# Moving the query normalisation from VectorE to ScalarE, a maximum to GpSimd, and re-timing a software-pipelined attention step

## The reference, cut to what matters

```python
def _layernorm(x, axis=-1, eps=1e-05):
    m = mean(x); v = var(x)
    return (x - m) / sqrt(v + eps)
...
scores = einsum('bhqd,bhkd->bhqk', q, k) * (1 / sqrt(16))   # q = layernorm(x), k = v = context
attn = softmax(scores, axis=-1)
out = einsum('bhqk,bhkd->bhqd', attn, v)
...
x = x + xattn(layernorm(x), ctx, ctx)
x = x + ffn(layernorm(x), w_gate, w_up, w_down)   # fp4_linear: w and x quantised by blocks of 16
```

## Time and profile before

| | |
|---|---|
| median of three timed runs | 544.02 us |
| profiled execution | 541.95 us, its span 540.2 us |
| TensorE clock granted, mean | 0.987 of full speed |
| busy: PE, weight loads | 494.7 us (92%), 396.8 us (73%) |
| busy: DVE, ACT, POOL | 453.2 (84%), 361.0 (67%), 269.9 us (50%) |
| chain that ended last | PE 57%, DVE 21%, issue 11%, SP queue 3% |

### The profile page before, as it was taken

How to read it: one execution, slowest core, us unless ns; L and a number is a source line. 1 busy time by engine, 2 the same in 40 slices (tenths; PEclk the granted TensorE clock), 3 DMA queues, 4 the chain that set the end, 5 groups by cost and what they waited for, 6 DMA issues and landing times.

```text
span 540.2 us, 13895 instructions
## 1 busy us (share of the span) xinstructions
PE 494.7 (92%) x4105; PEld 396.8 (73%) x4132; DVE 453.2 (84%) x1175; ACT 361.0 (67%) x707; POOL 269.9 (50%) x391
## 2 busy tenths in 40 slices
PE   3759999999999999999886799999999999999996
PEld 2326666666666666665454699999999999999996
DVE  3668999999999999989655788888998888898764
ACT  3227888888888888887683356666556666656653
POOL 5203444554444544433415466676666666666543
PEclk9999999999999999999995999999999999999999
DMA  6795545454455544440000000000000000000000
GB/s 197 195 222 146 143 137 148 121 156 131 134 149 156 142 131 138 118 118 2 4 1 0 2 12 21 21 19 16 13 19 19 19 19 19 10 19 20 21 21 30
DMA packets 43799, 40.63 MB, mean 75 GB/s; under 512 B 4728, under 2 KB 43512, under 8 KB 43768
## 3 DMA queue, kind: packets, MB, share of 16 engines
q1 hardware_dynamic: 43768, 40.26, 26.6%
HBM read 10.55 MB, written 4.19 MB: 27 GB/s over the span
## 4 chain that ended last, share of the span: by engine, by line
PE 57%; DVE 21%; issue 11%; SPq 3%; POOL 2%; DMA 2%; ACT 2%; DVEq 1%; POOLq 0%; ACTq 0%
PE SC L1086 21%; PE PV L1086 12%; DVE MF L678 12%; PE PV L1037 4%; PE SC L1005 4%; PE T L1111 4%; PE MX L1019 4%; PE T L1116 2%; DVE stats L686 2%; DVE QN L699 2%; PE T L988 1%; PE SC L1111 1%; DMA QS<-QP 1%; SPq L291 1%; DVE MP L708 1%
## 5 line engine op out<-in xcount | busy, mean ns | idle before, releaser
L678 DVE TENSOR_REDUCE MF<-MX 128x2 f32<-128x512 f32 x256 | 167.4, 684 | 18.3 <-PE MX L1019 17.7
L531 ACT ACTIVATE P<-SC 128x512 f32<-128x512 f32 x256 | 142.6, 605 | 25.3 <-PE SC L1005 24.4
L1019 PE MATMUL MX<-KS,QS 96*128 96x256 bf16 x512 | 103.8, 287 | 10.2 <-DMA QS<-QP 5.4
L1005 PE MATMUL SC<-QS,KS 98*128 98x256 bf16 x512 | 99.6, 277 | 0.2 <-DMA QS<-MT 0.2
L480 POOL TENSOR_TENSOR HQ<-HN,hscale 128x704 f32<-128x704 f32 x31 | 43.1, 1391 | 60.7 <-DVE HN L835 60.7
L1037 PE MATMUL PV<-P,VA 128*32 128x256 f32 x1024 | 69.4, 389 | 2.7 <-ACT OT L540 0.8
L1019 PEld LDWEIGHTS MX<-KS,QS 96*128 96x128 bf16 x512 | 47.0, 100 | 32.5 <-DVE MF L678 18.6
L610 ACT ACTIVATE HH<-T 128x768 fp32r<-128x768 f32 x31 | 25.2, 813 | 67.0 <-PE T L1111 67.0
L1005 PEld LDWEIGHTS SC<-QS,KS 98*128 98x128 bf16 x512 | 43.7, 98 | 33.7 <-ACT P L531 13.6
L1086 PE MATMUL SC<-WH,XH 128*128 128x352 f32 x256 | 68.1, 348 | 0.0
L1086 PE MATMUL SC<-WH,XL 128*128 128x352 f32 x256 | 62.5, 326 | 0.0
(11 more groups left out here) (134 smaller groups left out, 1018.8 us busy)
## 6 DMA issues: line engine op xcount, KB each, us to landing
KS<-KP SPq DMA_DIRECT2D x96, 128.0 KB, 2.4
QS<-QP SPq DMA_DIRECT2D x96, 128.0 KB, 2.4
X<-in_x SPq DMA_DIRECT2D x16, 256.0 KB, 2.8
C<-in_ctx SPq DMA_DIRECT2D x16, 256.0 KB, 3.1
out<-OB SPq DMA_DIRECT2D x32, 128.0 KB, 1.7
W<-in_L_ffn_w_down SPq DMA_DIRECT2D x1, 704.0 KB, 6.2
W<-in_L_ffn_w_gate SPq DMA_DIRECT2D x1, 640.0 KB, 4.5
W<-in_L_ffn_w_up SPq DMA_DIRECT2D x1, 640.0 KB, 4.9
```

Source lines behind the costliest of these rows:

```text
L531: nc.scalar.activation(P[g % 2][:, j, :, :], SC[h % 3][:, :, :], ACT.Exp, scale=0.25).then_inc(exp_done, 1)
L678: nc.vector.tensor_reduce(MF[st.slot(off, 2)][:, :, h:h + 1], MX[h % 2][:, :, :], AX.X, ALU.max, negate=True).then_inc(mx_done, 1)
L1005: last = nc.tensor.matmul(SC[h % 3][:, k, :], KS[r][0:ROWS, h, k * 128:(k + 1) * 128], QS[r][0:ROWS, h, :], start=True, stop=True)
L1019: last = nc.tensor.matmul(MX[h % 2][:, q, :], QS[r][0:PROD, h, q * 128:(q + 1) * 128], KS[r][0:PROD, h, :], start=True, stop=True)
```

## The change

ACT normalises x as scale * x + bias with scale `rstd` and bias `qbias` = -mean * rstd; POOL makes `nmean` and `qbias`. POOL takes the maximum of `WC` with the constant. Statistics move from head (0,1) to (0,3) on DVE, the split of the maxima from (2,2) to (2,1), the weights' scales from (2,3) to (2,0), the second output half from (3,2) to (3,3). ACT makes the keys' second part at (0,3), the queries' parts at (1,3), (2,2) and (3,3), and the two `OT` copies at (0,3) and (2,1). PE's transposes and two of its `PV` groups move with them.

```diff
@@ -150,6 +150,7 @@
         rstd = [sb(f"rstd{r}", [128, QT]) for r in range(2)]
+        nmean, qbias = sb("nmean", [128, QT]), [sb(f"qbias{r}", [128, QT]) for r in range(2)]
         MF = [sb(f"MF{r}", [128, QT, H]) for r in range(2)]
@@ -196,7 +197,7 @@
         consts = sem("consts")
-        ve_ready, rstd_ready, qn_ready = sem("ve_ready"), sem("rstd_ready"), sem("qn_ready")
+        ve_ready, rstd_ready, qbias_ready, qn_ready = (sem(n) for n in ("ve_ready", "rstd_ready", "qbias_ready", "qn_ready"))
         stats_seq, var_ready, kn_ready, neg_ready = (sem(n) for n in ("stats_seq", "var_ready", "kn_ready", "neg_ready"))
@@ -414,8 +415,11 @@
                     nc.gpsimd.tensor_scalar(ve[r][:, :], mv[:, :, 1], EPS, None, ALU.add).then_inc(ve_ready, 1)
-                    pool.wait_ge(ve_ready, st.times(LEAD, 1, 1))
+                    nc.gpsimd.tensor_scalar(nmean[:, :], mv[:, :, 0], -1.0, None, ALU.mult).then_inc(ve_ready, 1)
+                    pool.wait_ge(ve_ready, st.times(LEAD, 2, 2))
                     nc.gpsimd.tensor_tensor(rstd[r][:, :], ve[r][:, :], mhalf[:, :], ALU.pow).then_inc(rstd_ready, 1)
+                    pool.wait_ge(rstd_ready, st.times(LEAD, 1, 1))
+                    nc.gpsimd.tensor_tensor(qbias[r][:, :], nmean[:, :], rstd[r][:, :], ALU.mult).then_inc(qbias_ready, 1)
                 if st.has(1):
@@ -427,6 +431,9 @@
                     ws = wslice(st, GRID)
+                    pool.wait_ge(w_abs, st.times(GRID, 1, 1))
+                    gate(pool)
+                    nc.gpsimd.tensor_scalar(WC[:, :], WC[:, :], MAGIC * ONE, None, ALU.max).then_inc(w_c, 1)
                     pool.wait_ge(w_c, st.times(GRID, 1, 1))
@@ -521,6 +528,15 @@
+            def normalise(st, q):
+
+                r, b = st.slot(LEAD, 2), st.item(LEAD)
+                act.wait_ge(qbias_ready, st.times(LEAD, 1, 1))
+                act.wait_ge(q_tr, st.times(LEAD, 3))
+                gate(act)
+                nc.scalar.activation(QN[:, q, :, :, :], by_parity(X1[:, bass.ds(b * (QT * D) + q * D, D)]), ACT.Identity,
+                                     bias=qbias[r][:, q:q + 1], scale=rstd[r][:, q:q + 1]).then_inc(qn_ready, 1)
+
             def exp(st, g, j):
@@ -540,8 +556,11 @@
             def first_step(st):
-                for parts, bank, n, tr, out in ((KP, TA, 0, k_tr, k_out), (KP, TA, 1, k_tr, k_out), (QP, TB, 0, q_tr, q_out),
-                                                (KP, TA, 2, k_tr, k_out), (QP, TB, 1, q_tr, q_out), (QP, TB, 2, q_tr, q_out)):
+                part_out(KP[0], TA, 0, k_tr, k_out, st)
+                for q in range(QT):
+                    normalise(st, q)
+                for parts, bank, n, tr, out in ((KP, TA, 1, k_tr, k_out), (QP, TB, 0, q_tr, q_out), (KP, TA, 2, k_tr, k_out),
+                                                (QP, TB, 1, q_tr, q_out), (QP, TB, 2, q_tr, q_out)):
                     part_out(parts[0], bank, n, tr, out, st)
@@ -551,20 +570,26 @@
                         exp(st, g, j)
-                        for n, at in enumerate(((0, 3), (1, 1), (1, 2))):
-                            if (g, j) == at and st.has(LEAD):
-                                part_out(KP[st.slot(LEAD, 2)], TA, n, k_tr, k_out, st)
+                        if (g, j) == (0, 3) and st.has(LEAD):
+                            part_out(KP[st.slot(LEAD, 2)], TA, 0, k_tr, k_out, st)
+                        if (g, j) == (0, 3) and st.has(-1):
+                            evacuate(st, -1, 1)
                         if (g, j) == (0, 3) and st.has(GRID):
...
                             nc.scalar.activation(WC[:, :], wslice(st, GRID), ACT.Abs, scale=MAGIC).then_inc(w_abs, 1)
-                        if (g, j) == (0, 2) and st.has(-1):
-                            evacuate(st, -1, 1)
-                        for n, at in enumerate(((2, 1), (2, 3), (3, 3))):
+                        if (g, j) == (0, 3) and st.has(LEAD):
+                            part_out(KP[st.slot(LEAD, 2)], TA, 1, k_tr, k_out, st)
+                        if (g, j) == (1, 1) and st.has(LEAD):
+                            for q in range(QT):
+                                normalise(st, q)
+                        if (g, j) == (1, 2) and st.has(LEAD):
+                            part_out(KP[st.slot(LEAD, 2)], TA, 2, k_tr, k_out, st)
+                        if (g, j) == (2, 1) and st.has(0):
+                            evacuate(st, 0, 0)
+                        for n, at in enumerate(((1, 3), (2, 2), (3, 3))):
                             if (g, j) == at and st.has(LEAD):
                                 part_out(QP[st.slot(LEAD, 2)], TB, n, q_tr, q_out, st)
-                        if (g, j) == (3, 1) and st.has(0):
-                            evacuate(st, 0, 0)
                         if st.first == B - 1 and HG * g + j < LOTS:
@@ -682,6 +707,8 @@
                 dve.wait_ge(loaded[rc], st.turn(LEAD, RING, 32))
+                dve.wait_ge(ve_ready, st.times(LEAD, 2))
+                gate(dve)
                 for q in range(QT):
@@ -690,16 +717,6 @@
                     nc.vector.bn_aggr(mv[:, q, :], stats[:, q, :]).then_inc(stats_seq, 1)
-
-            def normalise(st, q):
-
-                r, b = st.slot(LEAD, 2), st.item(LEAD)
-                dve.wait_ge(rstd_ready, st.times(LEAD, 1, 1))
-                dve.wait_ge(q_tr, st.times(LEAD, 3))
-                nc.vector.tensor_scalar(QN[:, q, :, :, :],
-                                        by_parity(X1[:, bass.ds(b * (QT * D) + q * D, D)]),
-                                        mv[:, q, 0:1], rstd[r][:, q:q + 1],
-                                        ALU.subtract, ALU.mult).then_inc(qn_ready, 1)
@@ -762,10 +779,6 @@
-            def round_weights(st):
-                dve.wait_ge(w_abs, st.times(GRID, 1, 1))
-                nc.vector.tensor_scalar(WC[:, :], WC[:, :], MAGIC * ONE, None, ALU.max).then_inc(w_c, 1)
-
             def weights_out(n):
@@ -776,33 +789,26 @@
                         maximum(st, g, j)
-                        if (g, j) == (0, 1) and st.has(LEAD):
+                        if (g, j) == (0, 3) and st.has(LEAD):
                             statistics(st)
-                        if (g, j) == (0, 1) and st.has(LEAD):
                             aggregate(st)
...
                             weight_maxima(st)
-                        if (g, j) == (2, 3) and st.has(SCALE):
-                            weight_limits(st)
-                        if (g, j) == (3, 1) and st.has(SCALE):
-                            weight_inverses(st)
-                        if (g, j) == (1, 0) and st.has(LEAD):
-                            normalise(st, 0)
-                        if (g, j) == (1, 0) and st.has(LEAD):
-                            normalise(st, 1)
-                        if (g, j) == (2, 2) and st.has(1):
+                        if (g, j) == (2, 1) and st.has(-1):
+                            denominators(st, 0)
+                            output(st, 0)
+                        if (g, j) == (2, 1) and st.has(1):
                             maxima_high(st)
...
                             maxima_out(st)
-                        if (g, j) == (2, 1) and st.has(-1):
-                            denominators(st, 0)
-                            output(st, 0)
-                        if (g, j) == (3, 2) and st.has(-1):
+                        if (g, j) == (2, 0) and st.has(SCALE):
+                            weight_limits(st)
+                        if (g, j) == (3, 3) and st.has(-1):
                             denominators(st, 1)
                             output(st, 1)
-                        if (g, j) == (1, 3) and st.has(GRID):
-                            round_weights(st)
+                        if (g, j) == (3, 1) and st.has(SCALE):
+                            weight_inverses(st)
                         if st.first == B - 1 and HG * g + j < LOTS:
@@ -1063,10 +1069,10 @@
                         max_scores(st, g, j)
-                        for n, at in enumerate(((0, 3), (1, 1), (1, 3))):
+                        for n, at in enumerate(((0, 1), (1, 0), (1, 3))):
                             if (g, j) == at and st.has(LEAD):
                                 keys(st, n)
-                        for n, at in enumerate(((1, 3), (2, 3), (3, 2))):
+                        for n, at in enumerate(((2, 0), (2, 3), (3, 1))):
                             if (g, j) == at and st.has(LEAD):
@@ -1077,7 +1083,7 @@
                             transpose_weights(HG * g + j)
-                        if (g, j) == ((0, 2), (1, 1), (2, 2), (3, 3))[g]:
+                        if (g, j) == ((0, 3), (1, 1), (2, 1), (3, 3))[g]:
                             values(st, g)
```

## The result

The changed kernel takes 553.1 us (median of four runs, 551.53 to 558.46) against 544.12: a ratio of 1.0171, 95% interval 1.0131 to 1.0212. It is 9 us slower, where 540.6 was forecast and 536.0 to 546.0 given as the range. Its profiled execution took 552.0 us, 10.05 more than that of before.

The account below looks back on a forecast made before the run. DVE and PE were both nearly full, with the bound passing to PE: 14.33 + 0.39 + 0.04 = 14.76 us a step against 15.02, 0.26 x 13 = 3.4 us off, forecast 540.6 us, range 536.0 to 546.0.

Parts of the forecast that it names:

- What bounds the kernel: Attention step: DVE and PE nearly full, PE's own work 14.33 us, its two waits for DVE 0.69 us a step.
- ACT, what comes: Two QN activations on ACT between the exponentials of heads 5 and 6, taken at 0.49 us each, 0.98 a step.
- rival 2: ACT reads x's strided columns slowly, about 0.2 us more a pass: 15.15 us a step, 545.7 us; chance 0.1.
- The step laid out: Attention step timed from head 0's score pair: QN at 6.23, PV at 8.88 behind exponential 7, end at 14.76 us.
- POOL: nmean, qbias (0.22 us each) and the WC maximum (0.64 us) on POOL are covered, with 7.07 busy of 15.02 us.
- SP: Nothing added to SP's queue; the DMA of MT behind the keys' six lands at 14.4 to 14.6, before 14.76 us.
- rival 3: The DMA of MT behind the keys' stack becomes the bound: 0.51 us more a step, 550.6 us; chance 0.1.
- the ends: First items and last steps of the attention part: change taken as zero, 1 us either way.
- The chances: Outcomes for the whole kernel: faster (below 538.6 us) 0.3, slower (above 549.5) 0.1, within 1% 0.6.

Follow-up runs that it names:

- e12: Kernel before with the WC maximum still on DVE but two heads earlier, at (1,1) instead of (1,3): 541.3 us, ratio 0.9950.
- e4: Kernel before with only the WC maximum moved from DVE to POOL: 541.0 us, ratio 0.9943.
- e2: Changed kernel with ACT reading x and writing QN in x's own column order (query columns come out misordered): 549.2 us, ratio 1.0111.
- e8: Changed kernel with the queries' three parts later on PE and ACT: 557.3 us, ratio 1.0261.
- e1: Changed kernel with statistics and mv on DVE back at head (0,1): 546.0 us, ratio 1.0025.
- e7: e4 with the split of the maxima at (2,1) and the weights' scales at (2,0): 541.5 us, ratio 0.9942.
- e10: e4 with DVE's QN reading x in order and writing with gaps: 541.3 us, ratio 0.9930.
- e6: Changed kernel with QN back on DVE at (1,0) and statistics at (0,1): 543.4 us, ratio 0.9988.
- e5: Kernel before with only QN moved to ACT (nmean and qbias on POOL), behind exponential 4: 554.3 us, ratio 1.0195.
- e9: Changed kernel with statistics at (0,1) and ACT's QN reading x in order and writing with gaps: 544.1 us, ratio 0.9978.
- e11: e4 with QN shared, first half on DVE, second on ACT behind the keys' second part: 544.3 us, ratio 0.9995.

## Why the prediction was wrong, step by step

**What bounds the kernel.** PE's own work (14.33 us) was right, and the size of its two waits about right. Their cause was not: neither was DVE's load. The one ahead of the maxima's transposition was the `CAST` held up beside POOL (e12). The other, ahead of head 2's max pair, stays at 0.29 us in e4, with less work on DVE, and in the earlier trace rows DVE stands idle for 0.22 us ahead of the reduction that this pair waits for. The prediction's own intervals give it: max pair to reduction 0.42 and on to the pair two heads later 0.75 make 1.17, where PE needs 0.88. In the changed kernel it went because the keys' first transposition now stands between those pairs. So DVE, 96% busy, had next to nothing to give back in this step; both waits went by where the work stands.

**ACT, what comes: the mis-sized term, and the step that failed.** "I give `QN` the same 0.49, 0.98 a step." It is 1.45 (206.38 to 207.83), 811 ns at the median for one. I took the length from an activation over x in its own order, and kept the strided read as rival 2 with 0.1. Put right by itself (e2) this term is worth 0.43 us a step. The Trainium skill's rule that I set beside it (Advanced Engine Details and Errata, SBUF Cachelines) agrees in its direction with ACT in this case: 811 ns with 128 bytes between columns, 588 without (e2). My reason to doubt it was a row of DVE; what a row of one engine says of another was not tested. The rival's own size, 0.2 us a pass, was right (0.22), but its 15.15 us a step and 545.7 us were too low as well.

**The step laid out.** The head of the chain was good: statistics at 3.17 (3.17), `mv` at 4.07 (204.04, 4.07), `ve` 4.58 (4.59), `rstd` 5.06 (5.20), `qbias` 5.90 (6.00), `QN` 6.23 (6.41). So 0.18 of lateness is POOL's chain and the way from it to ACT, and 0.47 the length of `QN`. Carried down the path that I had laid out, by exponential 7 to `PV`, the two give 8.88 + 0.65 = 9.53 for `PV`, and it stands at 9.56 (209.53). The step then comes to 14.76 + 0.65 = 15.41, against 15.50 here and 15.59 on average; the last 0.1 to 0.2 I can't place. So the path was right and its terms were too short.

One wait I left out. Head 9's score pair at 7.59 without waits puts the transposition of `QN` at 7.16, and I didn't ask when `QN` is there: by my own numbers at 6.72 + 0.59 = 7.31. With those numbers it would have changed nothing, since head 9's pair had to wait for exponential 6 until 7.90. In the changed kernel `QN` ends at 207.92, 7.95 into the step, and PE goes at 8.01; the profile puts the 0.87 us down here. But exponential 6 holds head 9's pair to the same moment (207.83 and 0.69 make 208.52; it starts at 208.47), which is why e8 gained nothing. e1 and e2 take 0.56 and 0.43 us a step by themselves and 0.87 together, less than their sum.

**POOL.** Covered in sum, as said (8.37 us busy of 15.50), though `qbias` came 0.10 us later than laid out. That its passes would meet DVE's short operations I did not ask: `wscale` took 0.70 us in the changed kernel, just when ACT held PE up, so it is hidden there.

**SP, rival 3 and the ends.** In the steady steps the DMA of `MT` is in time, 213.04 against the score pair at 215.47. In the first full step it isn't; the chain of waits there:

```profile
49.64 0.81 ACT QN L537
...
50.93 0.49 ACT KP L529
...
51.65 0.60 SPq L292
...
55.69 2.36 DMA QS<-MT
```

`QN`, an exponential, the keys' third part, six issues, and then the DMA of `MT` with 2.36 us: the path of rival 3, here behind a late `QN`. The keys' issues start at 51.65 instead of 49.46 us. These 2.19, with the 0.49 by which the first DMA left earlier, are the 2.68 us of that step; the landing behind it makes PE wait once more, until 58.18. I had given the ends zero "and 1 us either way"; the first three steps together cost 5.0 us. How much of this is the change and how much the start of the DMAs stays open: the fourth DMA of `MT` leaves at 83.5 us before, at 88.1 in the changed kernel, and between 84.7 and 86.3 in the five kernels with `QN` on DVE alone, so that some 2 us of it may be chance of the start. The ends, taken at zero, are the second term that was mis-sized.

**The chances.** Slower got 0.1, and on the wrong mechanism; a faster outcome 0.3. Two questions would have turned it: what a pass with this access pattern costs on ACT, and whether DVE's load was what PE waited for.

No version tried beats e4, e7, e10 and e12, which lie at 0.993 to 0.995 and can't be told apart from one another. All four keep `QN` on DVE.

## What to carry to other kernels

When work moves to the engine that looks idle, lay out its list of instructions and ask of every later entry who waits for it; two idle microseconds in a step of fifteen took 1.5 us in one piece without loss in a steady step where it started early (e1 against e6), and not where its start was late or the next entry was due (the changed kernel, e5). Take the duration from a row with the same access pattern on the same engine, not from one with the same shape. Asking later for late work on an in-order engine did not repair it (e8): whoever waits for the next entry waits too. And look at short operations that last longer than they should beside another engine: moving one of 0.3 us by two heads (e12) gave 0.18 of the 0.29 us a step that taking it away gave (e4). A busy share of 96% did not mean that less work on that engine would shorten the step.

## What the runs showed of the hardware

- ACT, an activation over 128x256 fp32 with scale and bias from tiles: 588 ns in order (e2), 811 ns reading with 128 bytes between columns (834 in e1), 833 ns writing with 32 bytes between them (e9). DVE's `tensor_scalar` over the same data, strided on one side or the other: 505 and 524 ns (e4, e10), and 842 in e11, unexplained.
- DVE's `CAST` of 128x32 to bf16: 0.17 us alone, 0.43 us when a POOL pass over W was running, and both then end within 0.04 us of one another. The Trainium skill (SBUF — State Buffer, Who interferes with whom) says that DVE in some modes and GpSimd share one pair of ports as an exclusive lock; e12 agrees, and so does `wscale` at 0.70 us beside POOL's pass in the changed kernel. DVE's reductions of `MX` at 0.68 us show nothing of the kind.
